# Node layers that start on the first five tiles' folded sums, with two weights loaded a stage earlier and GpSimd's additions spread over the rounds

## The reference, cut to what matters

```
agg  = segment_sum(exp(e - max) * v[src], dst)        # attention sums, one row of 256 + 4 per node
rst  = agg / denom                                    # "res" in the kernel
skip = feat @ Wskip.T + bskip
g    = sigmoid(concat(skip, rst, skip - rst) @ Wgate.T + bgate)
rst  = layernorm(g * skip + (1 - g) * rst);  rst = where(rst >= 0, rst, a * rst)
x    = x + rst + ((out * gate) @ Wproj + bproj)       # "projected" and "bproj"
w    = softmax(layernorm(x) @ Wr + br)                # 8 experts per node
h    = relu(bn1(layernorm(x) @ W1[e]));  h = relu(bn2(h @ W2[e]))
x    = x + sum_e w[:, e] * (h @ Wo[e] + bo[e])
h_node = layernorm(x) @ W_node.T + b_node             # for the second graph layer
```

## Time and profile before

| | |
|---|---|
| median of 3 runs | 3103.57 us (3098.88 to 3108.4) |
| profiled execution | 3099.56 us, of which the span is 3097.9 us |
| PE busy | 2648.6 us (85% of the span) |
| DVE busy | 1979.6 us (64%) |
| ACT busy | 1370.0 us (44%) |
| POOL busy | 1067.3 us (34%) |
| mean granted PE clock | 0.939 |

### The profile page before, as it was taken

One profiled execution on the slowest core, in us unless ns is written; L12 is line 12 of the kernel. 1 busy time (PEld: TensorE's weight loads), 2 busy tenths in 40 slices (PEclk: granted clock), 3 DMA queues, 4 the chain that ended last, 5 costly groups with the idle time before them and its releaser, 6 DMA issues. The chain is left out here.

```text
span 3097.9 us, 54276 instructions
## 1 busy us (share of the span) xinstructions
PE 2648.6 (85%) x12024; PEld 2070.9 (67%) x12025; DVE 1979.6 (64%) x3898; ACT 1370.0 (44%) x2897; POOL 1067.3 (34%) x1184
## 2 busy tenths in 40 slices
PE   8776888729984999999988999999959987869698
PEld 6444555415543777777766888888848865647587
DVE  6676777868886443534225666666689977965411
ACT  2224323128861334333422444444469957846222
POOL 1577777721112000000005666666600006820043
PEclk9898999959996999999999999999979998989799
DMA  4799999937753000000007777777701113043254
GB/s 133 228 317 291 296 314 312 295 89 233 225 172 135 1 1 9 1 9 9 0 9 224 213 215 214 214 213 216 207 13 39 39 68 126 1 151 108 77 183 131
DMA packets 236589, 443.79 MB, mean 143 GB/s; under 512 B 29015, under 2 KB 128799, under 8 KB 235066
## 3 DMA queue, kind: packets, MB, share of 16 engines
q1 hardware_dynamic: 179516, 261.89, 27.2%
q0 software_dynamic: 56960, 180.47, 18.6%
HBM read 350.56 MB, written 92.69 MB: 143 GB/s over the span
## 5 line engine op out<-in xcount | busy, mean ns | idle before, releaser
L1879 PE MATMUL bank<-conv_w,conv_eT 128*128 128x256 f32 x2352 | 541.2, 380 | 4.6 <-DMA conv_eT<-in_edges 4.6
L1879 PEld LDWEIGHTS bank<-conv_w,conv_eT 128*128 128x128 f32 x2352 | 434.1, 190 | 56.6 <-DMA conv_eT<-in_edges 5.4
L1811 POOL DMA_INDIRECT conv_h<-table_h,conv_ix x392 | 384.5, 981 | 216.6 <-issue 115.3
L1576 ACT ACTIVATE area<-bank,nodes_bi,nodes_sc 128x320 f32<-128x320 f32 x320 | 197.5, 617 | 373.9 <-PE bank L1493 373.9
L667 POOL DMA_INDIRECT x<-table_qv,scores_ix x300 | 286.3, 954 | 182.6 <-ACT scores_ix L574 103.4
L1724 DVE SCALAR_TENSOR_TENSOR x<-bank,nodes_w,x 128x256 f32<-128x256 f32 x200 | 96.7, 484 | 319.5 <-PE bank L1502 319.5
L1835 DVE TENSOR_TENSOR conv_msg<-bank,conv_h 128x512 f32<-128x512 f32 x196 | 135.6, 692 | 192.9 <-PE bank L1879 192.9
L1343 PE MATMUL bank<-attend_pv,x 128*128 128x260 f32 x800 | 219.8, 403 | 26.6 <-POOL attend_pv L1274 24.5
L687 PE MATMUL bank<-sums,area 128*128 x800 | 228.0, 412 | 12.9 <-issue 5.7
L1343 PEld LDWEIGHTS bank<-attend_pv,x 128*128 128x128 f32 x800 | 137.0, 190 | 109.3 <-issue 62.6
L1778 ACT ACTIVATE conv_ix<-src 128x2 int32 x196 | 39.8, 203 | 367.4 <-DVE conv_msg L1835 344.6
(11 more groups left out here) (482 smaller groups left out, 5790.0 us busy)
## 6 DMA issues: line engine op xcount, KB each, us to landing
conv_eT<-in_edges SPq DMA_DIRECT2D x196, 384.0 KB
x<-edge_v SPq DMA_DIRECT2D x200, 256.0 KB, 3.0
edge_v<-x SPq DMA_DIRECT2D x150, 256.0 KB, 4.5
hidden_rows<-top_wide SPq DMA_DIRECT2D x25, 512.0 KB, 3.5
projected<-spline_hst SPq DMA_DIRECT2D x10, 960.0 KB, 4.4
ball_hT<-projected SPq DMA_DIRECT2D x5, 1920.0 KB, 18.6
top_wd<-in_top_wd SPq DMA_DIRECT2D x8, 1024.0 KB
x<-in_x SPq DMA_DIRECT2D x10, 640.0 KB, 9.1
```

The lines of the kernel that those rows point to most:

```text
L1576: nc.scalar.activation((h1, h2)[layer][:, o, hf * CW:(hf + 1) * CW], banks[n % HIDS][:, 0:CW], ACT.Relu, scale=sc[:, layer, e, o:o + 1], b ...
L1811: nc.gpsimd.indirect_dma_start(out=h[:, u, g, :], out_offset=None, in_=m.d_h, in_offset=bass.IndirectOffsetOnAxis(ap=ix[:, u * G + g:u * G ...
L1879: mm = nc.tensor.matmul(banks[u][:, g * F:(g + 1) * F], eT[:, u, g, c], w[:, c], start=False, stop=c == EC - 1, skip_group_check=True)
```

## The change

- The fold at the end of the attention sums covers only the first five tiles (`window_halves(0, U)`); the fold of the other twenty is done by DVE inside the node layers, in round -1: one half after the rows of `e` = 5, the other after the router's maximum at `e` = 7. SP issues the weights of experts 4 to 7 only after that (`merged`).
- `wskip` and `wproj` are loaded by SP at the start of the attention sums, into memory of the mix weights, which stays reserved until the node layers end. PE waits for no load at the start of the node layers; for the four other loads it waits ahead of the first logits. DVE waits for the two batch-norm tables alone, behind the first dots, where their five-step preparation (`norms_of_experts`) now stands.
- POOL adds the bias of chunk 0 as before, that of chunk p > 0 after `w_ready` p, which is at the start of round p-1; the clearing of chunk p-1 follows it.

```diff
@@ attention_sums
+                sp.dma_start(m.wskip, a["gnn_wskip"]).then_inc(vec_loaded, 16)
+                sp.dma_start(m.wproj, a["mix_wproj"]).then_inc(vec_loaded, 16)
...
-                merge_windows(nc, m, F + HEADS)
+                for at, to, odd in window_halves(0, U):
+                    nc.vector.tensor_tensor(m.sums[at, to], m.sums[at, to], m.sums[at, odd], ALU.add)
@@ node_layers, SP
-                for to, x in ((m.wskip, "gnn_wskip"), (raw[:, 0], "ffn_bn1"), (raw[:, 1], "ffn_bn2"), (m.wproj, "mix_wproj"), (m.wnode, "gnn1_wnode"),
-                              (wr[:], "ffn_wr"), (br[:], "ffn_br"), (bo[:], "ffn_bo")):
+                for to, x in ((raw[:, 0], "ffn_bn1"), (raw[:, 1], "ffn_bn2")):
+                    sp.dma_start(to, a[x]).then_inc(bn_loaded, 16)
+                sp.dma_start(m.x[:, tiles(0)], a["x"][0:CH].rearrange("(t p) f -> p t f", p=P)).then_inc(x_back[0], 16)
+                for to, x in ((wr[:], "ffn_wr"), (br[:], "ffn_br"), (bo[:], "ffn_bo"), (m.wnode, "gnn1_wnode")):
...
+                    if e == few:
+                        sp.wait_ge(merged, 1)
@@ node_layers, POOL
                 for p in range(TU):
                     pool.wait_ge(x_back[p], 16)
+                    if p:
+                        pool.wait_ge(w_ready, p)
                     nc.gpsimd.tensor_tensor(m.x[:, tiles(p)], m.x[:, tiles(p)], bproj.unsqueeze(1).to_broadcast([P, U, F]), ALU.add).then_inc(x_biased, 1)
-                for p in range(TU):
-                    pool.wait_ge(var_a, p + 1)
-                    nc.gpsimd.memset(m.sums[:, tiles(p)], 0.0)
+                    if p:
+                        pool.wait_ge(var_a, p)
+                        nc.gpsimd.memset(m.sums[:, tiles(p - 1)], 0.0)
+                pool.wait_ge(var_a, TU)
+                nc.gpsimd.memset(m.sums[:, tiles(TU - 1)], 0.0)
@@ node_layers, PE
-                pe.wait_ge(loaded, 16 * 8)
...
+                            if p == 0:
+                                pe.wait_ge(loaded, 16 * 4)
                             take(zs, p + 1)
@@ node_layers, DVE
-                dve.wait_ge(loaded, 16 * 8)
...
+                def norms_of_experts():
+                    dve.wait_ge(bn_loaded, 32)
...
+                def merge(k):
+                    at, to, odd = list(window_halves(U, NT))[k]
+                    c_(nc.vector.tensor_tensor(m.sums[at, to], m.sums[at, to], m.sums[at, odd], ALU.add))
...
                             dve.sem_inc(rows_b, 1)
+                            if p == 0:
+                                merge(0)
...
                                 dve.sem_inc(zs, 1)
+                                if p == 0:
+                                    merge(1)
+                                    dve.sem_inc(merged, 1)
```

More of the change, by code:

```diff
@@ L1184, in _, with window_halves @@
                     nc.vector.tensor_copy(m.probs[:, bass.ds(j, 1), :], got[:].unsqueeze(1)).then_inc(taken, 1)
+def window_halves(first, last):
+    half = P // 2
+    low, high = max(first, 1), min(last, NT - 1)
+    yield slice(0, half), slice(low, last), slice(NT + low - 1, NT + last - 1)
+    yield slice(half, P), slice(first, high), slice(NT + first, NT + high)
 def merge_windows(nc, m, wide):
@@ L1223, in _ @@
                         sp.dma_start(v[:, u], m.d_v[u % UN][:, bass.ds(i, G), :]).then_inc(arrived[u], 16)
-                sp.wait_ge(vec_loaded, 16 * 8)
+                sp.wait_ge(vec_loaded, 16 * 10)
             @block.scalar
@@ L1413, in node_layers @@
             st.sem(x) for x in ("var_c", "std_c", "rows_c", "turned_c", "kept_c", "h_made", "h_kept", "h_stored"))
-        steps_back = st.sem("steps_back")
+        steps_back, bn_loaded, merged = st.sem("steps_back"), st.sem("bn_loaded"), st.sem("merged")
         def rounds():
@@ L1434, in _ @@
             def _(sp):
-                for to, x in ((m.wskip, "gnn_wskip"), (raw[:, 0], "ffn_bn1"), (raw[:, 1], "ffn_bn2"), (m.wproj, "mix_wproj"), (m.wnode, "gnn1_wnode"),
-                              (wr[:], "ffn_wr"), (br[:], "ffn_br"), (bo[:], "ffn_bo")):
+                for to, x in ((raw[:, 0], "ffn_bn1"), (raw[:, 1], "ffn_bn2")):
+                    sp.dma_start(to, a[x]).then_inc(bn_loaded, 16)
+                sp.dma_start(m.x[:, tiles(0)], a["x"][0:CH].rearrange("(t p) f -> p t f", p=P)).then_inc(x_back[0], 16)
+                for to, x in ((wr[:], "ffn_wr"), (br[:], "ffn_br"), (bo[:], "ffn_bo"), (m.wnode, "gnn1_wnode")):
                     sp.dma_start(to, a[x]).then_inc(loaded, 16)
                 for e in range(XQ):
-                    if e < TU:
+                    if 0 < e < TU:
                         sp.dma_start(m.x[:, tiles(e)], a["x"][e * CH:(e + 1) * CH].rearrange("(t p) f -> p t f", p=P)).then_inc(x_back[e], 16)
+                    if e == few:
+                        sp.wait_ge(merged, 1)
                     for k, x in enumerate(("ffn_w1", "ffn_w2", "ffn_wo")):
@@ L1448, in _ @@
                         sp.dma_start(m.steps[0:1, :], m.d_steps).then_inc(steps_back, 16)
-                sp.wait_ge(loaded, 16 * 8)
+                sp.wait_ge(bn_loaded, 32)
+                sp.wait_ge(loaded, 16 * 4)
                 for e in range(XQ):
@@ L1614, in all_of @@
                     dve.wait_ge(own, c_.n)
-                dve.wait_ge(loaded, 16 * 8)
-                scv, biv = (t[:].rearrange("p l e c -> p l (e c)") for t in (sc, bi))
-                nc.vector.tensor_scalar(scv, raw[:, :, 4], BN_EPS, None, ALU.add).then_inc(std_bn, 1)
                 c_(nc.vector.tensor_tensor(gate_skip, gate_skip, gate_both, ALU.add))
                 c_(nc.vector.tensor_tensor(gate_res, gate_res, gate_both, ALU.subtract))
[L1620 to L1625, removed]
+                def norms_of_experts():
+                    dve.wait_ge(bn_loaded, 32)
+                    scv, biv = (t[:].rearrange("p l e c -> p l (e c)") for t in (sc, bi))
+                    nc.vector.tensor_scalar(scv, raw[:, :, 4], BN_EPS, None, ALU.add).then_inc(std_bn, 1)
+                    c_(nc.vector.tensor_tensor(biv, raw[:, :, 0], raw[:, :, 3], ALU.subtract))
+                    dve.wait_ge(std_bn, 2)
+                    c_(nc.vector.reciprocal(scv, scv))
+                    c_(nc.vector.tensor_tensor(scv, scv, raw[:, :, 1], ALU.mult))
+                    c_(nc.vector.tensor_tensor(biv, biv, scv, ALU.mult))
+                    nc.vector.tensor_tensor(biv, biv, raw[:, :, 2], ALU.add).then_inc(scales, 1)
+                def merge(k):
+                    at, to, odd = list(window_halves(U, NT))[k]
+                    c_(nc.vector.tensor_tensor(m.sums[at, to], m.sums[at, to], m.sums[at, odd], ALU.add))
                 def moments(k, src):
@@ L1663, in _ @@
                                                                       accum_out=dots[:, 1, u:u + 1]))
+                                if p == 0:
+                                    norms_of_experts()
                         if e == 1:
@@ L2793, in network @@
         m.wnode = m.area[:, 2 * U * F:2 * U * F + FT * F].rearrange("p (f n) -> p f n", f=FT)
-        m.wskip, m.wproj = (m.area[:, NP + 3 * U * F + k * FT * F:NP + 3 * U * F + (k + 1) * FT * F].rearrange("p (f n) -> p f n", f=FT)
-                            for k in range(2))
         m.mixed = m.rows[:].rearrange("p t f -> p (t f)").rearrange("p (c f n) -> p c f n", c=TU, f=FT)
@@ L2806, in network @@
         mix_ctx = ctx.enter_context(ExitStack())
-        m.wqT, m.wg1, m.wg2, m.bg1, m.bg2, m.mix_ln, m.context = (
+        m.wqT, m.wg1, both, m.bg1, m.bg2, m.mix_ln = (
             mix_ctx.enter_context(nc.sbuf_tensor(name, shape, F32)) for name, shape in (
-                ("wqT", [P, FT, F]), ("wg1", [P, FT, GH]), ("wg2", [GH, F]), ("bg1", [P, GH]), ("bg2", [P, FT]),
-                ("mix_ln", [P, 2, FT]), ("context", [P, FT, P])))
+                ("wqT", [P, FT, F]), ("wg1", [P, FT, GH]), ("mix_both", [P, 2 * F]), ("bg1", [P, GH]), ("bg2", [P, FT]),
+                ("mix_ln", [P, 2, FT])))
+        m.wg2 = both[0:GH, 0:F]
+        m.context = both[:, F:2 * F].rearrange("p (f n) -> p f n", f=FT)
+        m.wskip, m.wproj = m.wqT[:], both[:].rearrange("p (f n) -> p f n", f=FT)
         line_ctx = ctx.enter_context(ExitStack())
@@ L2829, in network @@
         recycle_semaphores(nc)
+        node_layers(nc, a, m, banks)
         mix_ctx.close()
-        node_layers(nc, a, m, banks)
         vec_ctx.close()
```

## The result

The changed kernel takes 3086.39 us (median of 8 runs, 3082.99 to 3094.38), the kernel before 3104.66 us (8 runs, 3098.88 to 3108.96): a ratio of 0.9944, interval 0.9933 to 0.9956, so 18.3 us or 0.56% faster. The forecast was 19.9 us off the median, 3083.7; its range was 3074 to 3092.

A forecast was written before the change was run, and what follows sets the result against it. The serial chain from 919 to 995 us, where PE hardly works, was taken as the bound, PE itself afterwards. 26.9 - 2.9 - 3.6 - 0.5 = 19.9 us off the 3103.57 median gives 3083.7 us, range 3074 to 3092.

The forecast's parts named there:

- The head: From the fold's start to the first expert: shorter fold, no wait for loads and less stretching by POOL gain 26.9 us.
- Round 0: At the first expert results: moved fold and POOL's addition delay division and dots, use up 5.19 us idle, cost 2.9 us.
- The bound of 4.1 us: Upper limit of the cost at the first expert results, if POOL's clearing also holds up the division's two-input instructions.
- Rounds 1 to 3: After each softmax, L129 waits for POOL's addition and L131 for its clearing; PE loses about 1.2 us each, 3.6 in all.
- DVE has 0.75 us of idle ahead of the first result: Slack in the later rounds, taken off some 2.0 us of DVE delay, leaving about 1.2 us of PE loss per round.
- The attention sums: At this stage's start, two moved loads issue ahead of the first edge values and delay them: 0.5 us, of 0 to 1.5.
- The weights of experts 4 to 7: Loads held until the fold is merged, some 7 us after the first expert begins; needed over 60 us after it: no cost.
- The rounds did not absorb the additions: Rival: POOL's work falls where DVE does not need the port; 0.5 to 1 us lost, about 3077.6 us; chance 0.17.
- they did not pay in full: Rival: every boundary pays its upper limit, 4.1 us first, then 3.3 each, attention start 1.5; 3092 us; chance 0.11.
- No other wait came into the head: Rival: DVE still starts 8.10 us late on another wait and boundaries pay in full; 3100 us; chance 0.06.
- the last rival: Stops at round starts drop PE to its lower clock, up to 15.2 us per boundary; 34 us slower, 3138; chance 0.04.

The follow-up runs named there:

- the loads back: Changed kernel with all eight loads again at the start of the node layers, PE and DVE waiting for all; 0.9966 of the kernel before.
- PE's wait alone: Changed kernel with the eight loads again at the node layers' start, PE waiting for all, DVE only before batch-norm preparation; 0.9960 of the kernel before.
- memory alone: Kernel before with only the changed kernel's memory layout, no instruction moved; 1.0001 of the kernel before.
- additions early: Changed kernel with POOL's five additions and five clearings put back where they stood before; 0.9949 of the kernel before.

## Why the prediction was right

- **The head.** 26.9 us were forecast, 26.8 came. Small errors cancelled: the two small folds took 2.75 us (forecast 2.50), POOL's addition began 6.9 us after the stage did instead of 5.9, 6.04 us after its DMA's issue began instead of 4.76 (the issue alone took 1.84 us instead of 0.38), and so it held up only the last batch-norm step. L1696 began 9.70 us after the stage did (forecast 9.95). The rest, 35.25 us, was read from the trace at 35.2. That the two agree to 0.1 us is luck, since the head of one code differs by up to 0.9 us between executions.
- **Round 0.** 2.9 forecast, 2.4 measured. The order was a little other: L1683 slipped in ahead of POOL (980.12 against 980.17) and the division waited, not the TENSOR_SCALAR before it. The bound of 4.1 us, with the clearing against two inputs, is ruled out as to its mechanism. The prediction gives 2.22 us for 0.17 as the row for two inputs; that row is the one-input L131, and the one for two inputs is L129, 1.12 us for 0.17.
- **Rounds 1 to 3.** 3.6 forecast, 4.2 measured. The mechanism was as told, L129 behind the addition and L131 behind the clearing, 1.05 and 0.71 us. The step that was off is "DVE has 0.75 us of idle ahead of the first result", taken for all three rounds: that idle stood in a round that PE began at clock 0.84. Round 3 before began at 1.00 and PE already stopped for 0.87 us there, so the same delay cost 1.7 us more of stop, and the change's rounds 1 and 3 began at 1.00. The nearness of 4.2 to 3.6 is luck in part. Rounds 1 to 3 of this code took 385.4 us in this execution and with the loads back, but 388.4 and 388.3 with PE's wait alone and in the change taken again; the rounds of before took 381.2 and 380.4 (memory alone). So the price lies between 4.2 and 8.0 us, and that of round 0, from the same traces, between 0.2 and 4.1.
- **The attention sums.** 0.5 forecast; 0.6 later at the fold, of which 0.38 stand at the first weighted pair (9.80 us after the stage's start instead of 9.42). Over all traces the four without the two early loads take 244.6 to 244.9 us for this stage, the nine with them 245.2 to 246.6, so 1.0 us is the fairer price. The weights of experts 4 to 7 cost nothing, as forecast: no wait of PE for them stands in the rounds.
- **The rivals.** The rounds did not absorb the additions, and they did not pay in full. No other wait came into the head. PE's clock did not fall after the stop of round 0 in this execution: the stretch from 973 to 1097 us has 0.99. It did behind three stops of the change taken again and behind two with PE's wait alone (4.46 and 4.36 us for the twelve matmuls). So the mechanism of the last rival exists, but at some 1.5 us a time and not the 15.2 us of a whole expert; the prediction's sum had it at nothing.
- **The sum.** -19.6 us in the touched stages, -18.3 in the medians; the interval of the ratio is 14 to 21 us. With means over all traces that run a stage as before or as changed, the head gives 26.5 us, rounds 0 to 3 cost 7.8 and the attention sums 1.0: -17.7 us. By these the forecast had the rounds 1.3 us too cheap (2.9 + 3.6 = 6.5), for the stops and the clock as told above, the attention sums 0.5 us too cheap, and the head 0.4 us too good.

## What to carry to other kernels

When a stage begins with loads and a long finish of the stage before it, split both by what the first tile needs, and put the rest where the engine is already waiting for another. A helper engine's read-modify-write is cheap only beside instructions that it does not hold up: release it by the event after which the other engine idles, not by the first event at which its data may be touched. Before idle time read from one round is spent in all of them, see whether the granted clock was the same in each, and read a stage's length from more than one execution.

## What was not expected

PE's clock falls for a moment at some round starts and not at others, in the same code: 0.84 over 11 us, a mean that mixes the two levels (1.2 and 2.4 GHz), directly behind ten matmuls on only 8 rows, which stand there in every round. The first sixteen matmuls of the round then take 6.26 us (1117.08, before) and not 4.57 (1371.70), 1.7 us, which hid the waits that the change made longer. In other executions it falls in the middle of a round, directly behind the router's twenty matmuls of 8 columns (additions early: these end at 1469.97, and the clock is 0.57 from 1470 to 1474 us, PE busy without a gap), or behind a stop, where it adds to the wait. What decides whether it falls stays open.
